# The pick table of a four-layer kernel: 128 products over 16 rows from reordered channel weights, with masks, parameter turn and angles placed later

## The reference

```python
W = weights[condition]                                   # layer 0: 16 matrices of 64x64, one chosen per sample
x = x + einsum('bct,bcd->bdt', x, W)
x = x + mask1 * (causal_conv(x, K1) + x * D1)            # layer 1: K1[h, l] from exponentials, cut at a length per sample
x = x + (x @ weight.T + bias + scale * lora(x, adapter)) # layer 2: over the time axis, 1024 x 1024, adapters of rank 16
x = x + mask3 * (causal_conv(x * mask3, K3) + mask3 * x * D3)  # layer 3: like layer 1
```

## Time and profile before

| What | Value |
|---|---|
| Median of 3 runs | 1706.78 us (1700.51 to 1707.58) |
| Profiled execution, its own time | 1704.94 us |
| Its span in the trace | 1703.1 us |
| Mean granted TensorE clock | 0.977 |
| TensorE busy | 1586.3 us (93%) |
| VectorE busy | 1034.2 us (61%) |
| ScalarE busy | 528.5 us (31%) |
| GpSimd busy | 823.9 us (48%) |
| DMA | 217.59 MB, mean 128 GB/s |

### The profile page before, as it was taken

The page is one execution under the profiler, slowest core; times in us unless marked ns, Lnnn a source line. Parts: engine busy times, 40 slices in busy tenths (PEclk is TensorE's granted clock), DMA queues, the critical chain, the costliest instruction groups (busy, mean ns, idle before and its releaser), DMA issues.

```text
span 1703.1 us, 30450 instructions
## 1 busy us (share of the span) xinstructions
PE 1586.3 (93%) x12055; PEld 1041.8 (61%) x12055; DVE 1034.2 (61%) x1349; ACT 528.5 (31%) x674; POOL 823.9 (48%) x365
## 2 busy tenths in 40 slices
PE   6876875999999999999999999999999999999996
PEld 6776764465656666565656565747474747474744
DVE  6777666746565656565656556666556565656532
ACT  2444343233232323232323232323232323232211
POOL 2000003617475656556565656564747473838334
PEclk9989888999999999999999999999999999999998
DMA  6799995335262625253535352526262625252314
GB/s 163 259 322 349 316 329 160 75 62 147 52 156 47 160 47 147 60 135 71 135 71 135 71 135 62 145 52 149 47 146 61 140 66 140 66 131 71 79 50 99
DMA packets 425955, 217.59 MB, mean 128 GB/s; under 512 B 337144, under 2 KB 412416, under 8 KB 423808
## 3 DMA queue, kind: packets, MB, share of 16 engines
q1 hardware_dynamic: 409728, 177.45, 41.9%
q10 hardware_dynamic: 16192, 39.67, 6.3%
HBM read 94.98 MB, written 71.76 MB: 98 GB/s over the span
## 4 chain that ended last, share of the span: by engine, by line
PE 83%; DMA 6%; DVE 6%; issue 3%; ACT 1%; POOL 0%; SPq 0%; POOLq 0%; DVEq 0%; ACTq 0%
PE ps L745 39%; PE ps L784 7%; PE ps L675 7%; DMA arena<-in_x_dram 6%; PE ps L710 5%; PE ps L737 5%; PE ps L753 5%; PE ps L797 3%; PE ps L618 3%; PE ps L679 3%; PE ps L727 2%; PE ps L565 2%; PE ps L723 1%; DVE arena L1514 1%; DVE arena L1520 1%
## 5 line engine op out<-in xcount | busy, mean ns | idle before, releaser
L745 PE MATMUL ps<-arena,w2t 128*128 128x512 f16 x3072 | 681.3, 379 | 0.0
L745 PEld LDWEIGHTS ps<-arena,w2t 128*128 128x128 f16 x3072 | 300.5, 98 | 362.3
L532 POOL TENSOR_TENSOR arena<-arena 128x1024 f32<-128x1024 f16 x64 | 151.1, 2361 | 550.9 <-DMA arena<-arena 533.5
L508 POOL TENSOR_TENSOR arena<-arena 128x1024 f32<-128x1024 f32 x32 | 72.6, 2269 | 306.1 <-DMA arena<-tab_scratch 244.2
L1520 DVE TENSOR_SCALAR arena<-ps,biasx 128x512 f32<-128x512 f32 x128 | 94.3, 747 | 208.1 <-ACT arena L1079 207.8
L1079 ACT ACTIVATE arena<-ps,biasx 128x512 f16<-128x512 f32 x128 | 87.1, 687 | 424.1 <-PE ps L753 424.1
L618 PE MATMUL ps<-arena 128*128 128x128 f32 x1024 | 148.4, 308 | 49.7 <-DMA arena<-in_x_dram 29.7
L618 PEld LDWEIGHTS ps<-arena 128*128 128x128 f32 x1024 | 139.2, 219 | 56.9 <-issue 28.3
L710 PE MATMUL ps<-arena 128*128 128x512 f16 (+1 forms) x768 | 138.8, 332 | 7.3 <-DVE arena L1439 7.3
L784 PE MATMUL ps<-arena 128*128 128x256 f16 (+1 forms) x1536 | 138.3, 247 | 3.2 <-DVE arena L1514 3.0
L535 POOL TENSOR_TENSOR arena<-arena,one_xs 128x1024 f32<-128x1024 f32 x64 | 136.0, 2125 | 5.0
(11 more groups left out here) (215 smaller groups left out, 2181.8 us busy)
## 6 DMA issues: line engine op xcount, KB each, us to landing
arena<-in_x_dram SPq DMA_DIRECT2D x64, 512.0 KB, 8.8
out_dram<-arena SPq DMA_DIRECT2D x64, 512.0 KB, 3.0
gbuf<-x_scratch SPq DMA_DIRECT2D x120, 256.0 KB, 3.7
arena<-krow_scratch SPq DMA_DIRECT2D x32, 512.0 KB, 4.5
x_scratch<-arena ACTq DMA_DIRECT2D x14, 1024.0 KB, 9.2
x_scratch<-arena ACTq DMA_DIRECT2D x14, 896.0 KB, 8.6
arena<-tab_scratch SPq DMA_DIRECT2D x32, 200.0 KB, 2.6
w2t<-in_L_cond_weight_dram ACTq DMA_DIRECT2D x8, 512.0 KB, 3.2
```

The source lines that it names most:

```text
L532: nc.gpsimd.tensor_tensor(past[:, h % 2].rearrange("p (k t) -> p k t", k=NBLK), x3t[:, h % 2, 0], x3t[:, h % 2, 1], ALU.add).then_inc(past ...
L745: nc.tensor.matmul(ps[:, 4 + o % 3, :], w2t[:, o, part, k, :], xx[:, :, k, :], start=(k == 0 and q == 0), stop=False)
```

## The change

The channel weights are loaded once, into 16 partitions, in four transfers of a quarter of the columns each. VectorE adds 1 on the diagonal and copies them, in eight pieces of 8 output channels (`w0p`), into an order in which the 64 input channels of one output channel lie next to each other; the two memsets go. TensorE makes two products per output channel, one for the even and one for the odd samples: 64 weight columns, 16 rows, 64 moving columns of `onehot` (now [16, 128], every second column), results in PSUM partitions 0 to 63 and 64 to 127. It waits before each group for that group's copy. GpSimd clears `pick` in eight pieces, and ScalarE waits for the eighth. The masks are made behind the parameters, before stage0, and ScalarE waits for them before its first copy into the second half of `xq`. In the first half round the turn of the parameters moves from step 1 to step 2 on all three engines, and the three angle pieces from steps 1, 2, 3 to 2, 3, 4.

```diff
-        w0n = area(56, 32)
+        w0n = area(56, 16)
+        w0p = area(72, 16).rearrange("p (d c) -> p d c", d=C)
...
         tcoli = small[:, 24:32].bitcast(I32)
-        onehot = sb("onehot", [4 * NID, PAIRS], F32)
+        onehot = sb("onehot", [NID, B], F32)
         zrow = sb("zrow", [P, P], F32)
...
             sp.dma_start(len3i, len3.rearrange("(b o) -> b o", o=1)).then_inc(ids_loaded, 16)
-            for copy in range(4):
-                q = copy // 2
-                sp.dma_start(w0n[NID * copy:NID * (copy + 1), q * C * C:(q + 1) * C * C],
-                             w0.rearrange("i c d -> i (c d)")).then_inc(w0_loaded, 16)
+            for quarter in range(4):
+                cols = slice(quarter * (C * C // 4), (quarter + 1) * (C * C // 4))
+                sp.dma_start(w0n[0:NID, cols], w0.rearrange("i c d -> i (c d)")[:, cols]).then_inc(w0_loaded, 16)
...
-            nc.gpsimd.memset(area(0, 32), 0.0).then_inc(pick_cleared, 1)
+            for piece in range(8):
+                nc.gpsimd.memset(area(4 * piece, 4), 0.0).then_inc(pick_cleared, 1)
...
-            pe.wait_ge(w0_ready, 2)
-            src = w0n[0:4 * NID, :].rearrange("i (m d) -> i d m", d=C)
+            src = w0p[0:NID]
             for dgroup in range(8):
+                pe.wait_ge(w0_ready, dgroup + 2)
                 for e in range(8):
-                    mm = nc.tensor.matmul(ps[:, dgroup, e * PAIRS:(e + 1) * PAIRS], src[:, 8 * dgroup + e, :],
-                                          onehot[:, :], start=True, stop=True)
+                    for q in range(2):
+                        mm = nc.tensor.matmul(ps[q * C:(q + 1) * C, dgroup, e * PAIRS:(e + 1) * PAIRS], src[:, 8 * dgroup + e, :],
+                                              onehot[:, :].rearrange("i (n q) -> i q n", q=2)[:, q, :], start=True, stop=True)
                 mm.then_inc(pick_summed, 1)
...
                     if first and k == 0:
-                        if step == 1:
+                        if step == 2:
                             turn_params()
...
-            act.wait_ge(pick_cleared, 1)
+            act.wait_ge(pick_cleared, 8)
             for dgroup in range(8):
...
+                    if first and m == STEPS + 3:
+                        act.wait_ge(masks_ready, NBLK + 1)
                     if m >= 3:
...
                         load_scale(step)
-                        if step == 1:
+                        if step == 2:
                             copy_turned()
...
-            for q in range(2):
-                nc.vector.memset(w0n[2 * NID * q:2 * NID * (q + 1), (1 - q) * C * C:(2 - q) * C * C], 0.0)
             dve.wait_ge(iota_done, 3)
...
             link(nc.vector.tensor_copy(pcol, pcoli))
-            pair_ids = idf[:, 0, :].rearrange("p (n q) -> p q n", q=2)
-            ts(onehot[0:2 * NID], pair_ids[0:2 * NID, 0], pcol[0:2 * NID, :], None, ALU.is_equal)
-            ts(onehot[2 * NID:4 * NID], pair_ids[2 * NID:4 * NID, 1], float(2 * NID), pcol[2 * NID:4 * NID, :], ALU.add, ALU.is_equal)
+            ts(onehot[:, :], idf[0:NID, 0, :], pcol[0:NID, :], None, ALU.is_equal)
             dve.wait_ge(w0_loaded, 64)
-            for q in range(2):
-                own = w0n[2 * NID * q:2 * NID * (q + 1), q * C * C:(q + 1) * C * C]
-                own = bass.AP(own.tensor, own.offset, [own.ap[0], [C + 1, C]])
-                ts(own, own, 1.0, None, ALU.add).then_inc(w0_ready, 1)
+            diag = w0n[0:NID, 0:C * C]
+            diag = bass.AP(diag.tensor, diag.offset, [diag.ap[0], [C + 1, C]])
+            ts(diag, diag, 1.0, None, ALU.add).then_inc(w0_ready, 1)
+            dve.wait_ge(w0_ready, 1)
+            for dgroup in range(8):
+                cols = slice(8 * dgroup, 8 * dgroup + 8)
+                nc.vector.tensor_copy(w0p[0:NID, cols], w0n[0:NID, :].rearrange("i (c d) -> i d c", d=C)[:, cols]).then_inc(w0_ready, 1)
             nc.vector.tensor_copy(tcol, tcoli)
...
             nc.vector.tensor_copy(steps[:, TB:TB + TL], trow[:, 0:TL * TB].rearrange("p (l s) -> p l s", s=TB)[:, :, 0])
-            for k in range(NBLK):
-                ts(mask1[:, k, :], idf[:, 1, :], tcol[:, k:k + 1], None, ALU.is_gt).then_inc(masks_ready, 1)
-            ts(past3[:, :], trow[:, :], len3f, None, ALU.is_ge).then_inc(masks_ready, 1)
...
             ts(d_row[:, :], prm[0:TB, 320:448], 1.0, last_row, ALU.add, ALU.mult).then_inc(params_ready, 1)
+            for k in range(NBLK):
+                ts(mask1[:, k, :], idf[:, 1, :], tcol[:, k:k + 1], None, ALU.is_gt).then_inc(masks_ready, 1)
+            ts(past3[:, :], trow[:, :], len3f, None, ALU.is_ge).then_inc(masks_ready, 1)
...
                     if first and k == 0:
-                        if step == 1:
+                        if step == 2:
                             turned_bias()
...
                             split_k(blk - 1)
-                    if step == 1:
+                    late = 1 if first and k == 0 else 0
+                    if step == 1 + late:
                         right_angles(blk, k, i)
-                    if step == 2:
+                    if step == 2 + late:
                         left_angles(blk, k)
-                    if step == 3:
+                    if step == 3 + late:
                         adv_angles(blk, k)
...
                         combine_a(blk, k)
```

## The result

The changed kernel takes 1696.69 us (median of 20 runs, 1692.61 to 1702.31) against 1706.65 (median of 20 runs, 1700.51 to 1709.77) on the same chips: a ratio of 0.9946, 95% interval 0.9937 to 0.9955. The profiled execution took 1696.3 us, with a span of 1694.1, 9.0 less than before.

A forecast was written before the change was run, and what follows sets the result against it. It took a start chain (weight loads, pick products, x products, parameters) ahead of a transfer-bound stage to bound the kernel; 1704.94 - 9.6 = 1695.3 us for the profiled execution, 1697.2 against the median; range 1690 to 1705.

The forecast's parts named there:

- Weights: Start of the kernel: the four smaller channel weight loads are in place at 9.7 us, before at 15.5.
- POOL's pieces: GpSimd's clearing of pick in eight pieces at the start: holds VectorE for one piece at most, counted as nothing.
- Copies and parameters: VectorE's start: eight copies at 0.6 us each, 4.8 in all; parameters start at 16.2 us, before 19.30.
- Products: TensorE's pick: 256 records, 106 ns each for 7 us, then 66 at the upper clock; 19.5 us, ending at 30.1.
- Rival 1: Pick products stay at the lower clock, 106 to 110 ns a record; gain 4.3 us, time 1702.5; chance 0.20.
- Rival 2: Pick records still cost 220 ns, so 256 take 56.3 us; slower, 1730.6 us; chance 0.10.
- limit of 123 ns: Price per pick record above which the change was said to lose time.
- ScalarE: Start: angles ready at 26.1 us, sines done at 29.4, parameters at 38.5; last pick groups copied by 33.0.
- Masks and ScalarE's wait: Masks (2.2 us) paid once, behind the sines, made at 40.7 us; ScalarE's wait for them at m = 19 costs nothing.
- Step shift: Transposes, turned bias and angles one step later: same work in shifted order; turned bias at 43.6, 9.6 us sooner.
- The x stage: The transfer-bound x products behind the start: keep the whole 9.6 us gain, with bounds of 0 and 9.6.
- Rival 3: Transfers leading from 75 us on swallow half of the gain; time 1702 us; chance 0.08.

The follow-up runs named there:

- the kernel with ScalarE's clearing: Against the changed kernel, GpSimd clears five of the eight pieces of pick and ScalarE the last three; single time 1696.55 us.
- the probe: Against the changed kernel, four 128x128 float32 products of the identity with itself added behind pick group 3, to read TensorE's clock; single time 1695.22 us.
- parities in turn: Against the changed kernel, each group's eight products for even samples come first, then the eight for odd ones; single time 1700.59 us.
- the second profile: The changed kernel run once more with nothing changed, on another set's chip; 1695.63 us, ratio 0.9942 to the kernel before.

## Why the prediction was right

The time was right to 0.5 us (1697.2 against 1696.69), and so was the place of the gain, with two of its steps wrong in ways that nearly cancelled. That it came within 0.5 us is luck: the twenty runs of the changed kernel spread over 10 us.

- *Weights.* Forecast in place at 9.7; the last was issued at about 4.5 and took some 4.9, and in the kernel with ScalarE's clearing the diagonal, which waits for them alone, started at 9.48. Right.
- *POOL's pieces.* "It can hold a VectorE operation for a piece, no longer for all" failed. The cast stood for 2.83 us until the last piece was done and the diagonal started at 10.77, 1.3 us late. I had the earlier trace rows only from 16 us on; the term was put at nothing with no row behind it, and VectorE's cast at 9.50 in the kernel before, shown above, spoke against it.
- *Copies and parameters.* 0.53 us a copy (forecast 0.6), and the parameters' own loads landed by 12.4, sooner than the 16.5 that I let weigh in. With the cast's 1.3 us against these, the parameters started at 16.20, forecast 16.2: right by cancellation.
- *Products.* Forecast to be no longer last, at 7 us of 106 ns and then 66 by a risen clock. They were not last, for another reason. The clock stayed at 1.2 GHz (the probe), a record there costs 86 ns and not 106 (parities in turn), and neighbours in the two halves overlap, 54 ns. The forecast named this overlap beside the sum and put no time on it; the runs make it the mechanism, though it was not needed: at 86 ns the products ended at 33.8, and the turned bias came only 0.84 us later than in the changed kernel's profile. Rival 1 had the right clock and the wrong price. Rival 2 was far: the record fell from 220 to 54. Its limit of 123 ns is worked out wrong: the 4.3 us belong to records of 110 ns, so the sum gives 127.
- *ScalarE.* Sines forecast at 29.4; done at 28.04 and used at 28.72. ScalarE loaded its table at 21.70, while it waited for the angles, so that 1.3 of the 3.3 us went aside. VectorE, busy until 28.68 with work that needs no sines, did not wait for them.
- *Masks and ScalarE's wait.* Paid once, behind the sines, and no gain from it: right, by the kernel with the masks ahead. The x steps 0 to 3 were sooner too, as the groups 5 to 7 ended at 31.7 (forecast 33.0). The turned bias, forecast at 43.6, came at 43.55, by luck: the parameters ended 0.7 us sooner than forecast, and the transposes, at the lower clock in this profile, took that back. In the second profile it was 42.88.
- *Step shift.* "The work that follows is the same in an order shifted by a step" failed, by about 3 us as the medians have it: TensorE's idle 2.73 us before the transposes was in the sum (I had m = 5 wait for the copy), but I compared it with the old start and not with the shift left out, and I missed the longer wait at lot B and the fall of the granted clock with it. In the forecast's own terms 0.9 us of the 9.0 were lost between the turned bias and the first wait for x, where the forecast had counted 0.7 more, for the odd copy already done.
- *The x stage.* Counted to keep all; 9.0 us were there at its end, against 8.95 at the turned bias. Rival 3 did not happen.

The gain of 0.54% lies just over the 0.5% that the chances turned on, and its interval (0.45 to 0.63%) takes that in; this is why those of faster and of no change stood so near each other.

## What to carry to other kernels

When a long producer leaves the chain, the sum of the next chain is what counts: write down every instruction of the engine that becomes last, and ask of each of them whether it could stand in a hole further on. Small clearing jobs on GpSimd held VectorE's cast for as long as they followed each other; end them before VectorE has its input, or give them to an idle ScalarE (it made the start sooner here; a time saved by it alone was not seen). A step moved "for order" must be priced against leaving it in place, not against the old kernel, and a longer pause of TensorE is to be looked at together with the clock granted behind it.

## What the runs showed of the hardware

- GpSimd's eight memsets of 128x1024, one behind the other, held a VectorE cast of 128x384 from 7.64 until they had ended at 10.26 (2.83 us, against 0.36 without them). Cutting the memset in eight did not let the cast in between. A VectorE memset of 32x4096 was not held by a GpSimd memset (3.47 us, from 6.01 to 9.48).
- Float32 products of 16 rows, 64 weight columns and 64 moving columns at 1.2 GHz take 86 ns a record when neighbours write to the same half of the output partitions and 54 when they alternate between halves; reported durations (219 and 303 ns) are the same in both and tell nothing of the pace.
- The same records with weights read in steps of 256 bytes take 75 ns, alternating.
- The granted clock is printed as 1.00 over a stretch whose durations are those of 0.50, in the start of these profiles (the probe at 18.7 us; the x products at 31.7 have 421 ns too); a few products of known duration placed there tell which it is.
- ScalarE loaded the table for its sine before the semaphore that the sine waits for (21.70, where the sine started at 26.16). It is no rule: the load for the first pick copy, at 13.71 in the same profile, began only when that copy's products were done.
- Around TensorE's idle 2.95 us before L604 the granted clock fell to 0.50 in all eight profiles that have it, and stayed 1.00 in the four where the idle was 1.26. The 2.73 us before m = 5 were followed by 0.50 in the first profile of the changed kernel (42 to 45), the 1.92 us in the second by 1.00.
